# GpSimd forms partial sums of the softmax probabilities, the rotation's products and most residual additions in an adaLN transformer block

## The reference, cut to what matters

```python
mod = (silu(c) @ wmod).reshape(2, 6, 1, -1)          # shifts, scales and gates
h = layernorm(x) * (1 + ca) + sa                      # x: 2 x 1024 x 512
# attention: 16 query heads of 32, one key head and one value head shared by all
q = rmsnorm(apply_rope(h @ Wq.T)); k = rmsnorm(apply_rope(h @ Wk.T)); v = h @ Wv.T
#   apply_rope(x) = x * cos + concat([-x2, x1]) * sin
attn = softmax(where(causal, q @ k.T * 32**-0.5, -inf))
x = x + ga * (rmsnorm(attn @ v) @ Wo.T)
h = layernorm(x) * (1 + cb) + sb
# mixture of experts: 64 experts, 8 of them for each token, and one shared MLP
x = x + gb * (experts(h) + shared_mlp(h))
```

## Time and profile before

| | |
|---|---|
| median of 3 runs | 1260.75 us (1259.95 to 1263.04) |
| profiled execution: its own time | 1264.72 us |
| its span, first to last instruction | 1262.9 us |
| mean granted TensorE clock | 0.962 |
| busy: PE, PEld, DVE, ACT, POOL | 91%, 69%, 78%, 60%, 39% |

### The profile page before, as it was taken

The page is one execution under the profiler, slowest core; times in us unless marked ns, Lnnn a source line. Parts: engine busy times, 40 slices in busy tenths (PEclk is TensorE's granted clock), DMA queues, the critical chain, the costliest instruction groups (busy, mean ns, idle before and its releaser), DMA issues.

```text
span 1262.9 us, 25455 instructions
## 1 busy us (share of the span) xinstructions
PE 1149.0 (91%) x8828; PEld 875.0 (69%) x8828; DVE 990.5 (78%) x1903; ACT 753.4 (60%) x1497; POOL 495.3 (39%) x375
## 2 busy tenths in 40 slices
PE   8989999999998888999897999999999999999940
PEld 4545556555565655555556989999999999999930
DVE  4678786766548888685567798999999989999968
ACT  3456555556665434555644367787777778787720
POOL 1213211121122212011010127878878887887740
PEclk9999999989999879999999999999999999999975
DMA  9570000000000000002014149999999999999968
GB/s 351 175 277 1 1 18 2 9 10 2 22 2 9 10 13 10 1 21 83 22 42 133 55 149 267 297 300 300 298 297 298 299 296 299 298 300 298 295 176 282
DMA packets 77166, 189.93 MB, mean 150 GB/s; under 512 B 11496, under 2 KB 12136, under 8 KB 76832
## 3 DMA queue, kind: packets, MB, share of 16 engines
q1 hardware_dynamic: 44256, 112.01, 26.1%
q0 software_dynamic: 28672, 71.32, 23.2%
q10 hardware_dynamic: 4160, 5.58, 1.2%
HBM read 136.36 MB, written 52.51 MB: 150 GB/s over the span
## 4 chain that ended last, share of the span: by engine, by line
PE 63%; DVE 14%; DMA 6%; issue 5%; DVEq 5%; POOL 4%; ACT 3%; POOLq 0%; SPq 0%; ACTq 0%
PE ps L1249 17%; PE ps L1288 9%; PE ps L1070 8%; PE ps L1055 4%; PE ps L1098 4%; PE ps L991 4%; PE ps L1023 4%; DMA acc_dram<-y,slots 4%; PE ps L1235 3%; DVE nmax L1491 3%; POOL acc_dram L665 3%; PE ps L1040 2%; PE ps L963 1%; PE ps L1085 1%; POOL xg L650 1%
## 5 line engine op out<-in xcount | busy, mean ns | idle before, releaser
L665 POOL DMA_INDIRECT acc_dram<-y,slots x128 | 250.0, 1953 | 80.2 <-issue 48.6
L1491 DVE TENSOR_REDUCE nmax<-ps 128x1 f32<-128x512 f32 (+3 forms) x304 | 191.6, 657 | 94.5 <-PE ps L1027 53.2
L774 ACT ACTIVATE probs<-ps 128x512 f32<-128x512 f32 (+1 forms) x320 | 159.2, 554 | 88.1 <-PE ps L1055 87.0
L616 POOL TENSOR_SCALAR_AFFINE_SELECT probs<-probs 128x512 f32<-128x512 f32 x64 | 44.4, 695 | 382.1 <-ACT probs L774 382.0
L650 POOL DMA_INDIRECT xg<-h_dram,slots x128 | 129.5, 1012 | 107.5 <-DVE slots L1682 49.1
L1023 PE MATMUL ps<-kpad,qpT 128*128 128x512 f32 (+3 forms) x384 | 148.5, 455 | 13.6 <-DVE nmax L1491 11.6
L1249 PE MATMUL ps<-x_hi,e_gu_hi 128*112 128x256 f32 (+1 forms) x768 | 120.1, 278 | 0.0
L1249 PE MATMUL ps<-x_hi,e_gu_lo 128*112 128x256 f32 (+1 forms) x768 | 119.6, 278 | 0.0
L1055 PE MATMUL ps<-qT,kT 98*128 98x512 f32 (+1 forms) x320 | 114.6, 436 | 5.0 <-ACT probs L774 4.8
L1249 PE MATMUL ps<-x_lo,e_gu_hi 128*112 128x256 f32 (+1 forms) x768 | 110.2, 279 | 1.5 <-DVE x_lo L1693 1.2
L1693 DVE TENSOR_TENSOR e_gu_lo<-e_gu,e_gu_hi 128x1408 fp32r<-128x1408 f32 x64 | 104.0, 1624 | 8.8 <-issue 6.0
(11 more groups left out here) (222 smaller groups left out, 2361.4 us busy)
## 6 DMA issues: line engine op xcount, KB each, us to landing
e_gu<-in_gate_up SPq DMA_DIRECT2D x64, 704.0 KB
e_d<-in_w_down SPq DMA_DIRECT2D x64, 224.0 KB
acc_dram<-h SPq DMA_DIRECT2D x2, 4608.0 KB, 25.8
e_d<-in_w_down SPq DMA_DIRECT2D x64, 128.0 KB
wmod_b<-in_wmod SPq DMA_DIRECT2D x2, 2048.0 KB, 22.1
xg<-h_dram SPq DMA_DIRECT2D x16, 256.0 KB, 3.3
acc_a<-acc_dram SPq DMA_DIRECT2D x8, 512.0 KB, 11.5
acc_b<-acc_dram SPq DMA_DIRECT2D x8, 512.0 KB, 7.5
```

The costliest lines, as they stand in the source:

```text
L665: pool.indirect_dma_start(out=acc_dram[a], out_offset=bass.IndirectOffsetOnAxis(ap=slots[:, at:at + 1], axis=0), in_=y[e % 2][:, h, :], in ...
L774: act.activation(probs[:, n % PROBS, 2 * pr:2 * pr + 2, off:CW], unit_bank(2 * n + pr)[:, :, off:CW], ACT.Exp).then_inc(s_exp, 1)
L1491: dve.tensor_reduce(nmax[:, 1 if lo else 0, first:first + heads], max_view(n, heads, hi - lo), AX.X, ALU.max, negate=True).then_inc(s_max, 1)
```

## The change

1. **Partial sums.** In each group, POOL adds up the probabilities of all key tiles but the last two (DIRECT) into a new tile `part_sum` (`add_probs`: 128 x 1024, one addition for each of kt = 1 to keys - 3). PE multiplies `part_sum` by ones once, and the last two key tiles directly; the products with ones of the others go. That is for chunks with 4, 6 and 8 key tiles; those with 2 are as before.
2. **Rotation.** The three products move from DVE's `rotate` to POOL (`rotate_products`), for all 16 tiles. DVE keeps the sum of squares and the addition.
3. **Residual additions** of tiles 0 to 11 (POOL_ADDS) move from DVE to POOL (`residual_add`).
4. **Buffers.** `xn` and `sq` share one tile, so ACT's `squares` moves behind the next tile's `modulate` and `normalise` waits for DVE's sum of squares two tiles back. `scratch` becomes a slot of `h2`, so the wait for that slot's store and turn moves from `shift` to `residual` and `mean_square`.
5. **New waits.** `exponentials` waits until the buffer that it writes has been added (`s_sum`), `values` of the last pair waits for the group's last addition, the first addition of a group waits until the group before has been multiplied (`s_pv`), POOL's products wait for DVE's split of the tile before (`s_parts`), and its residual addition for DVE's scaling (`s_atd`).

```diff
+DIRECT = 2
+POOL_ADDS = 12
...
-        xn = sb(att, "xn", [P, D])
+        xn_sq = sb(att, "xn_sq", [P, H + 1, HD])
+        xn, sq = xn_sq[:, 0:H, :].rearrange("p h d -> p (h d)"), xn_sq
...
+        part_sum = sb(att, "part_sum", [P, GH, CW])
...
+        def added(q):
+
+            return max(0, keys(q) - 1 - DIRECT)
...
-              "key_value_out": -27, "query_out": -23, "squares": -22, "rotate": -15, "head_rms": -11, "split": -9,
+              "key_value_out": -27, "query_out": -23, "squares": -20, "rotate_products": -18, "rotate": -13, "head_rms": -11, "split": -9,
...
+            def add_probs(q, g, kt):
+                n = step_of(q, g, kt)
+                if kt == 1:
+                    pool.wait_ge(s_pv, (n - 1) // 2)
+                pool.wait_ge(s_exp, 2 * n + 2)
+                pool.drain()
+                before = probs[:, (n - 1) % PROBS, :, :] if kt == 1 else part_sum[:, :, :]
+                pool.tensor_tensor(part_sum[:, :, :], before, probs[:, n % PROBS, :, :], ALU.add).then_inc(s_sum, 1)
+
+            def rotate_products(t):
+                i = t % TPB
+                shape = [P, H + 1, half]
+                pool.wait_ge(s_kve, t + 1)
+                pool.wait_ge(s_qk, t + 1)
+                if t:
+                    pool.wait_ge(s_parts, t)
+                pool.tensor_tensor(t1[:, :, :], qk[:, :, :], cos[:, i, :].unsqueeze(1).to_broadcast([P, H + 1, HD]), ALU.mult)
...
+            def residual_add(t):
+                xt = xtile(t)
+                pool.wait_ge(s_atd, t + 1)
+                pool.tensor_tensor(xt, xt, h2[:, t % 2, :], ALU.add).then_inc(s_xadd, 1)
...
+                for tile, n in tile_due(m, "residual", 2):
+                    if n == 1 and tile < POOL_ADDS:
+                        residual_add(tile)
+                for tile, _ in due(m, "rotate_products"):
+                    rotate_products(tile)
+                for q, g, kt in steps_at(m):
+                    if 1 <= kt <= added(q):
+                        add_probs(q, g, kt)
...
+                    q0, g0, kt0 = all_steps[n - PROBS]
+                    if kt0 <= added(q0) and added(q0):
+                        act.wait_ge(s_sum, sums_to(q0, g0, max(kt0, 1)))
...
-                for at in (0, CW):
-                    for kt in (2 * k, 2 * k + 1):
-                        off = first_query(q, kt)
-                        for j in range(GH):
-                            last = pe.matmul(ps[HD * j:HD * j + HD, PV_BANK, at + off:at + CW],
-                                             v_sb[:, b, kt, :] if at == 0 else ones[:, :],
-                                             probs[:, (n + kt % 2) % PROBS, j, off:CW], start=(kt == 0 and at == 0),
-                                             stop=(kt == keys(q) - 1 and at == CW))
+                for kt in (2 * k, 2 * k + 1):
+                    off = first_query(q, kt)
+                    for j in range(GH):
+                        last = pe.matmul(ps[HD * j:HD * j + HD, PV_BANK, off:CW], v_sb[:, b, kt, :],
+                                         probs[:, (n + kt % 2) % PROBS, j, off:CW], start=(kt == 0), stop=False)
+                if k == last_pair and added(q):
+                    pe.wait_ge(s_sum, sums_to(q, g, added(q)))
+                    for j in range(GH):
+                        pe.matmul(ps[HD * j:HD * j + HD, PV_BANK, CW:2 * CW], ones[:, :], part_sum[:, j, :], start=False, stop=False)
+                for kt in (2 * k, 2 * k + 1):
+                    if added(q) and kt <= added(q):
+                        continue
+                    off = first_query(q, kt)
+                    for j in range(GH):
+                        last = pe.matmul(ps[HD * j:HD * j + HD, PV_BANK, CW + off:2 * CW], ones[:, :],
+                                         probs[:, (n + kt % 2) % PROBS, j, off:CW], start=False, stop=(kt == keys(q) - 1))
                 last.then_inc(s_pv, 1)
```

More of the change, by code:

```diff
@@ L275, in build_program @@
         s_kv, s_kve, s_exr, s_posr = (sem("s_" + n) for n in ("kv", "kve", "exr", "posr"))
-        s_gb = sem("s_gb")
+        s_gb, s_sum, s_turned, s_xadd = (sem("s_" + n) for n in ("gb", "sum", "turned", "xadd"))
         s_pack_k, s_qp = sem("s_pack_k"), sem("s_qp")
@@ L306, in adds_before @@
             return sum(accumulator(k) == a for k in range(e))
+        half = HD // 2
         def xtile(t):
@@ L364, in steps_at, with sums_to @@
             return found
+        all_steps = [(q, g, kt) for q in range(NCHUNK) for g in range(NG) for kt in range(keys(q))]
         def step_of(q, g, kt):
             return steps_before(q) + g * keys(q) + kt
+        def added(q):
+            return max(0, keys(q) - 1 - DIRECT)
+        def sums_to(q, g, kt):
+            return sum(NG * added(k) for k in range(q)) + g * added(q) + min(kt, added(q))
         def masks_before(q, g, kt):
@@ L441, in build_program @@
         CHUNK_AT = {"gram": 11, "mean_square": 11, "row_rms": 12}
-        FIRST_AT = {"project": 12, "residual": 16, "rstd": 18, "shift": 21, "turn": 23, "rows": 23, "logits": 25,
+        FIRST_AT = {"project": 12, "residual": 16, "rstd": 19, "shift": 21, "turn": 23, "rows": 23, "logits": 25,
                     "out": 25}
-        SECOND_AT = {"project": 26, "residual": 27, "rstd": 29, "shift": 30, "turn": 35, "rows": 35, "logits": 36,
+        SECOND_AT = {"project": 26, "residual": 27, "rstd": 30, "shift": 32, "turn": 35, "rows": 35, "logits": 36,
                      "out": 37}
@@ L1512, in mean_square @@
                 dve.drain()
+                if q == 0:
+                    dve.wait_ge(s_init, 48)
+                else:
+                    dve.wait_ge(s_h2_out[0], 16 * q)
+                    dve.wait_ge(s_h2t, CT * q - 1)
                 for j in range(CT):
-                    dve.tensor_tensor_reduce(scratch[:, j * P:(j + 1) * P], ps[:, gram_bank(q), j * P:(j + 1) * P], ident, 1.0, 0.0,
+                    dve.tensor_tensor_reduce(h2[:, 0, j * P:(j + 1) * P], ps[:, gram_bank(q), j * P:(j + 1) * P], ident, 1.0, 0.0,
                                              ALU.mult, ALU.add, oms[:, j:j + 1])
@@ L1527, in residual @@
                     dve.wait_ge(s_at, t + 1)
[L1528 to L1532 removed]
+                    if t >= 2:
+                        dve.wait_ge(s_h2_out[slot], 16 * (t // 2))
+                        dve.wait_ge(s_h2t, t - 1)
+                    scratch = h2[:, slot, :]
+                    dve.scalar_tensor_tensor(scratch, ps[:, tile_bank(t), :], orstd[:, q % 2, j:j + 1], ga[:, t // TPB, :],
+                                             ALU.mult, ALU.mult).then_inc(s_atd, 1)
+                    if t >= POOL_ADDS:
+                        dve.drain()
+                        dve.tensor_tensor(xt, xt, scratch, ALU.add)
+                elif n == 2 or t >= POOL_ADDS:
+                    if t < POOL_ADDS:
+                        dve.wait_ge(s_xadd, t + 1)
                     dve.bn_stats(st2[:, slot, :], xt)
@@ L1733, in _ @@
                     mean_square(q)
-                for tile, n in tile_due(m, "residual", 2):
-                    residual(tile, n)
+                for tile, n in tile_due(m, "residual", 3):
+                    if n != (1 if tile < POOL_ADDS else 2):
+                        residual(tile, n)
                 for tile, _ in tile_due(m, "shift"):
                     shift(tile)
-                for tile, n in due(m, "rotate", 4):
+                for tile, n in due(m, "rotate", 2):
                     rotate(tile, n)
```

42 lines of the change are left out of this document (13 added, 29 removed).

## The result

The changed kernel takes **1324.05 us** (1321.37 to 1329.75, 4 runs); the kernel before, beside it, 1261.89 (1259.95 to 1266.03, 4 runs). The ratio is **1.049, 95% interval 1.045 to 1.054**: 5% slower, where 1250 was predicted, and beyond the range's end of 1275. The profiled execution has a time of 1321.37 us and a span of 1319.5, with a granted clock of 0.936 (before: 0.962).

The account below looks back on a forecast made before the run. PE was taken to bound chunks with 6 and 8 key tiles, PE with DVE the others. Chunk terms -2 - 5 - 9 - 5 + 10 = -11 us gave a median of 1250, range 1233 to 1275.

Parts of the forecast that it names:

- It stays covered, barely: Attention chunks: DVE's busy time plus waiting stays below PE's: 73 of 77 us in chunk 3, 67 of 78 in 2.
- "+5" for the routing: End of chunk 7: DVE's routing meets five additions of the last group at 1 us each; chunk total +10 us.
- PE's 33.5 us, if nothing else comes to bind: Attention, both sequences: PE saves 72 products with ones, 1.9, 5.6 or 9.3 us per chunk of 4, 6, 8 key tiles.
- the price of a product: Attention: one key tile's product with ones on PE is 8 instructions and takes 0.465 us.
- The loop on POOL: Groups of 8 key tiles: additions, selects and PE's last pair form a 15.5 us cycle, 62 us per chunk.
- the forecast's 5: Chunk 7: POOL's cycle and its giving way make 72 us against PE's 67, so +5 us.
- The slower rival: Additions take 2.52 us and each gives way 0.59; POOL's cycle lengthens chunks 3, 7; +16 us to 1277; chance 0.30.
- if DVE turns into the bound in chunks 2, 5 or 6: Attention: a listed sign that the forecast is wrong, DVE setting the pace in those chunks; no size given.
- DVE's gain: Moved rotation products and residual additions free DVE of 3.4 to 4.7 us per chunk; 1 us counted in chunks 0 and 4.
- Shared buffers: Tile preparation: sharing `xn`/`sq` and using `h2` for `scratch` only moves waits, at no cost.
- my upper bound of 2.52: POOL's partial-sum addition of 128 x 1024 takes at most 2.52 us, priced as four selects; lower bound 1.06.
- my 2.2: POOL's partial-sum addition of 128 x 1024 was taken to last 2.2 us, between 1.92 and 2.52.

Follow-up runs that it names:

- run 1: The changed kernel without partial sums: PE multiplies every key tile by ones again; moved products, residual additions and shared buffers stay; 1258.99 us, ratio 0.996.
- run 3: The changed kernel with each partial-sum addition replaced by a 13-element power of about 2.48 us on POOL, all waits kept; 1254.69 us, ratio 0.9928.
- run 5: The changed kernel without additions or waits for them; PE's instructions stay, one product taking a probabilities tile instead of the sum; 1242.34 us, ratio 0.9827.
- Run 10: The changed kernel without partial sums and with residual additions back on DVE; the rotation's products stay on POOL; 1257.13 us, ratio 0.9939.
- run 9: The changed kernel without partial sums, rotation's products and residual additions back on DVE; only buffers and order remain changed; 1260.94 us, ratio 0.9971.

## Why the prediction was wrong

The lengths of the chunks' stretches, from the first exponential of one to that of the next (chunk 7's to the end of its last):

| | 0 | 1 | 2 | 3 | 4 | 5 | 6 | 7 |
|---|---|---|---|---|---|---|---|---|
| before | 42.7 | 69.0 | 84.5 | 85.2 | 61.6 | 81.2 | 72.7 | 66.7 |
| 1: no additions | 45.3 | 67.1 | 81.5 | 85.2 | 61.1 | 78.7 | 70.3 | 67.3 |
| 5: PE's saving alone | 44.1 | 65.7 | 77.7 | 78.3 | 61.0 | 79.7 | 67.7 | 67.8 |
| 3: long powers | 45.2 | 65.4 | 78.2 | 78.6 | 60.6 | 78.9 | 67.8 | 70.0 |
| changed kernel | 45.2 | 70.0 | 83.7 | 95.0 | 60.5 | 87.1 | 79.3 | 98.1 |

As medians the steps are: before 1263, without additions 1259, with PE's saving 1242, with POOL's 2.48 us in the loop 1255, with POOL's passes over SBUF 1324.

**The step that failed: "It stays covered, barely".** I had added 1.3 us of DVE waiting for each addition and compared the sum with PE's busy time: 73 of 77 us in chunk 3, 67 of 78 in chunk 2. The waiting was mis-sized a little: DVE's busy time is 81.0 in chunk 3, 29 us over run 1's 51.7 or 1.5 for each of 20 additions, 67.1 in chunk 2, and in chunk 7 77.4 for 42.6, 1.7 for each of 20. The comparison was what failed. Chunk 2, forecast right at 67, has DVE busy for 80% of the stretch and is still 5.5 us longer than in run 3, which has no blocking; chunk 5, at 75.6 us of busy time near the forecast's 74, is 8.2 us longer with only four additions. DVE works in a fixed order, and so do PE and ACT behind it; where DVE stands for 2 us ahead of a reduce or of a piece of the routing, they stand too, whatever its share of busy time says. The list of waits of the changed kernel, from 81 to 701 us, shows it beside the earlier trace rows:

```profile
PEld ps L1082 <- DVE nmax L1541: 36.9, 53, 3.2
...
PE ps L1082 <- DVE nmax L1541: 21.4, 20, 2.9
...
PE ps L1099 <- DVE qs L1552: 18.3, 9, 4.6
...
PE ps L1216 <- ACT hot_row L875: 13.1, 3, 6.8
PE ps L1152 <- DVE oT L1558: 12.7, 4, 7.0
```

PE's waits for `row_max` went from 11.6 to 21.4 us, and new ones stand beside them: `qs` of the split, `oT` of the last chunk, and `hot_row`, which ACT could only finish once DVE had made it.

**Chunk 7: "+5" for the routing, in all +10.** It was +31. The forecast charged only the last group's five additions, at 1 us each; they held these operations for 12.5 us, where run 3 takes 2.0. The other three groups' additions meet `hot`, the division, the last residual additions and the routing's first half, which I had left out although showed the chain going through that half. In chunk 7 the operations with 512 elements of `hot_row` take 981 ns on average against 422 in run 1, and the division `oT` 1642 against 414.

**"PE's 33.5 us, if nothing else comes to bind."** In run 5 nothing of POOL binds, and 16.7 us come. Chunk 3 gives 6.9 of 9.3, chunk 2 3.8 of 5.6, chunk 7 nothing. The products were saved in all of them (stretches of chunks 3 and 7, first in run 1, then in run 5):

```profile
277.00:362.00 85.00, 82.53 (x786) 49.91 (x786) 51.66 (x135) 55.44 (x125) 22.16 (x24) 1.00 0.03 9
572.00:640.00 68.00, 62.88 (x675) 37.09 (x677) 42.78 (x137) 44.10 (x92) 7.22 (x11) 0.95 0.06 19
```

```profile
269.00:348.00 79.00, 76.54 (x629) 45.76 (x628) 51.76 (x136) 56.33 (x128) 23.21 (x24) 0.98 0.03 10
556.00:624.00 68.00, 56.90 (x523) 33.48 (x521) 42.96 (x136) 43.91 (x92) 6.95 (x10) 0.92 0.08 28
```

So two things are in the missing half. One is the size of the term: PE's busy time over the eight stretches fell by 22.6 us (514.9 to 492.3), not by 33.5. In chunk 3 it fell by 6.0 us, at a granted clock of 0.98 where run 1 had 1.00; run 3, at 1.00 there, is 8.8 us below run 1, so the price of a product was nearly right and a lower clock took part of the gain. In chunks 1, 2, 3 and 6 the stretches shrank about as much as PE's busy time. The other is chunk 7: PE's busy time fell by 6.0 us and the stretch by nothing.

PE is busy for 97% of the stretch in chunk 3 but for 84% in chunk 7. There the chain of run 5 passes for 11 us through DVE alone, released by ACT and going on to PE's `place`:

```profile
581.34 1.27 ACT sh_gu_hi L877
582.63 1.63 DVE sh_gu_lo L1745
...
585.53 0.75 DVE h L1582
...
593.15 0.44 DVE hot_row L1717
...
594.87 0.62 ACT hot_row L871
595.54 1.11 PE ps L1211 x8
```

The 93% of the earlier trace rows meant that PE had little slack for more work. It did not mean that less PE work shortens the stretch: by this view DVE's chain is as long as PE's there. The earlier trace rows had DVE's chain at two other places, at the start and the end of this stretch, and I had used it only for the price of additions. That the chain explains all of chunk 7's missing gain is read from this view; it wasn't tried apart.

**The loop on POOL.** Right in its parts: five additions take 12.6 us (forecast 11.5), their starts lie 2.5 to 2.7 apart (forecast 2.3, with DVE's operations 2.6). Run 3 shows it without the blocking. Chunk 3 is 0.3 us longer than in run 5 and chunk 7 2.2, less than the forecast's 5, but the powers of the last group are not done when the last exponentials are. In the chain of run 3 behind chunk 7 stand

```profile
629.68 2.43 POOL part_sum L643
632.11 1.19 POOL probs L631 x2
633.34 1.51 PE ps L1131 x16
...
643.23 8.47 PE ps L1168 x16
```

PE waits 7.0 us for the last select, and its last projection then takes 8.47 us where it took 6.88 in the earlier trace rows. From the last exponentials to ACT's first work on an expert's weights it is 92.0 us, against 84.0 in run 5. The forecast had this place in the loop but not behind the chunk. In the changed kernel it doesn't show (85.6), since the exponentials were late themselves.

**The slower rival** had chance 0.30 and gave 1277. Its sign came true, its mechanism did not: it put the cost on POOL's lateness, from 2.9 us between two additions; the spacing stayed below that. No rival let DVE's chain become the bound, though the signs to look for named it ("if DVE turns into the bound in chunks 2, 5 or 6").

**DVE's gain.** I gave it 1 us each in chunks 0 and 4, and a little in 1 and 5. Run 10 shows 3.8 us over run 9 for the rotation as a whole, about that size. The work behind it was mis-sized: in chunk 3 DVE has eight operations fewer in run 1 than in the earlier trace rows, 4.7 us by the forecast, and its busy time is not shorter (51.66 us, 51.35 before). With the moved work on POOL, operations that stayed on DVE take longer: the cast `qs<-nmax` of 16 elements takes 420 ns on average in the eight stretches of run 1 and 183 before. **Shared buffers** at no cost: they brought 3.9 us (run 9). Its profiled execution has the same span as that of before (1262.8 and 1262.9), so where they lie is not seen and stays open.

The 48 additions of 2.42 and 24 of 2.45 us lie nearest to my upper bound of 2.52. The Trainium skill (GPSIMD Engine Reference, § Performance versus the Vector engine) gives 4497 ns for 2048 elements, half of which, 2.25 us as an estimate, is a little nearer than my 2.2; by neither would the forecast have changed its sign.

## What to carry to other kernels

Before wide passes go to GpSimd, don't add their length to VectorE's busy time and compare with the bound: count the passes, and ask for each which VectorE operation stands at that place and who waits for it in order, and take that operation as ending when the pass ends. Here that was 1 us of kernel time for each of 72 additions of 2.4 us, and more where VectorE runs a chain of small dependent operations.

A stretch in which the busiest engine is at 93% can still be bound by two chains of equal length: if the chain that ended last passes through another engine for 10 us, don't count on the busiest engine's saving there. Running the saving alone, with the work that pays for it left out, shows this in one run.

## What the runs showed of the hardware

**What GpSimd's passes block.** VectorE's groups over the attention of the changed kernel (mean ns behind the busy time):

```profile
L1541 DVE TENSOR_REDUCE nmax<-ps 128x1 f32<-128x512 f32 x192 | 127.9, 683 | 49.0 <-PE ps L1082 39.5 <-PE ps L1086 7.9
L1558 DVE TENSOR_TENSOR oT<-oT,sums_s 128x256 f32<-128x256 f32 x31 | 28.2, 911 | 2.7 <-ACT sums_s L846 2.7
...
L1524 DVE TENSOR_TENSOR t<-t,wkq 128x32 f32<-128x32 f32 x13 | 11.1, 852 | 0.0
L1587 DVE SCALAR_TENSOR_TENSOR h<-ps,orstd,mods 128x512 f32<-128x512 f32 x14 | 10.5, 751 | 5.4 <-issue 2.8 <-PE ps L1165 2.6
L1523 DVE CAST qs<-t 128x512 fp32r<-128x512 f32 x13 | 10.1, 774 | 1.2
...
L1595 DVE BATCH_NORM_STATS2 st<-xres 128x6 f32<-128x512 f32 x14 | 9.7, 694 | 3.6 <-POOL xres L661 2.7
```

The same groups without additions (run 1):

```profile
L1541 DVE TENSOR_REDUCE nmax<-ps 128x1 f32<-128x512 f32 x192 | 127.9, 684 | 54.9 <-PE ps L1082 46.1 <-PE ps L1086 7.0
...
L1558 DVE TENSOR_TENSOR oT<-oT,sums_s 128x256 f32<-128x256 f32 x31 | 13.6, 438 | 1.9 <-ACT sums_s L846 1.9
...
L1587 DVE SCALAR_TENSOR_TENSOR h<-ps,orstd,mods 128x512 f32<-128x512 f32 x14 | 10.5, 750 | 11.7 <-PE ps L1165 9.6 <-issue 2.0
...
L1595 DVE BATCH_NORM_STATS2 st<-xres 128x6 f32<-128x512 f32 x14 | 9.7, 694 | 2.7 <-POOL xres L661 1.7
...
L1523 DVE CAST qs<-t 128x512 fp32r<-128x512 f32 x13 | 5.6, 434 | 1.2
...
L1524 DVE TENSOR_TENSOR t<-t,wkq 128x32 f32<-128x32 f32 x13 | 2.4, 184 | 0.0
```

Operations with two SBUF inputs are held, down to 32 elements a partition (0.184 to 0.852 us on average), but so is a cast with one input (0.434 to 0.774), which my sum had not counted, and the scalar operation `ms<-ssq`, one input of 17 elements (0.176 to 0.429 over the 16 tiles). Reduces and operations that read PSUM beside one SBUF tensor, and the statistics, keep their time within a nanosecond. The Trainium skill (SBUF — State Buffer, § Who interferes with whom) names casts among the operations that can take the shared port; the trace agrees.

**Not every long GpSimd operation blocks.** The power of 13 elements (2.48 us) leaves DVE's small operations at 0.17 to 0.23 us, and DVE's busy time in chunk 3 at 50.2 us (51.7 without additions).

**The clock.** In chunk 7 of the changed kernel the granted clock is 0.80 as a mean (0.97 in the earlier trace rows, 0.95 with powers), so the engine spent part of the stretch at the lower of its two levels, 1.2 GHz instead of 2.4. PE was idle for 36 us there, in waits up to 11.8 us. At 641.5, 651.8 and 689.3 us the clock fell from 1.00 to 0.50, each time while PE stood in one of its longest waits (5.5, 6.8 and 11.8 us). Its 520 matmuls took 62.8 us; 521 took 55.4 in the run with powers. I put these 7 us down to the lower clock; no run separates them from the waiting.
